# Two sum passes of a graph kernel: the edge weights move from VectorE's one-hots to ScalarE's multiply of the gathered rows

## The reference, cut to what matters

```python
# layer 1: edge_index = (row, col), 7 edge types
index = row * 7 + edge_type
mean = segment_sum(x[col], index, N * 7) / maximum(count of index, 1)[:, None]
out = mean.reshape(N, -1) @ weights
# layer 2:
h = x @ W
deg = segment_sum(ew, col, N);  dinv = where(deg > 0, rsqrt(deg), 0)
norm = dinv[row] * ew * dinv[col]
out = segment_sum(h[row] * norm[:, None], col, N) + bias
```

## Time and profile before

| | us |
|---|---|
| median of 3 runs | 9,699.5 |
| lowest, highest | 9,695.85, 9,704.59 |
| span of the profiled execution | 10,401.4 |
| of it: pass "sum1" | 3,755 to 5,010 |
| of it: pass "sum2" | 5,545 to 6,803 |
| busy: TensorE, VectorE, GpSimd, ScalarE | 6,311.5, 4,856.6, 4,458.2, 2,031.2 |

### The profile page before, as it was taken

One profiled execution on the slowest core, in us unless ns is written; L12 is line 12 of the kernel. 1 busy time (PEld: TensorE's weight loads), 2 busy tenths in 40 slices (PEclk: granted clock), 3 DMA queues, 4 the chain that ended last, 5 costly groups with the idle time before them and its releaser, 6 DMA issues. The chain is left out here.

```text
span 10401.4 us, 95746 instructions
## 1 busy us (share of the span) xinstructions
PE 6311.5 (61%) x28050; PEld 4795.7 (46%) x28050; DVE 4856.6 (47%) x13537; ACT 2031.2 (20%) x5038; POOL 4458.2 (43%) x4412
## 2 busy tenths in 40 slices
PE   0001115999996865454665444453965788887699
PEld 0000004888884433333443333342863676776466
DVE  7561216888884532222242222264113566666633
ACT  0000002444443210000120000012212232232322
POOL 0546772666660036666104666602020566664000
PEclk9998557999997986666676666675987777777799
DMA  0001002333330133333102333301960232222000
GB/s 12 6 1 28 7 4 71 83 83 83 83 83 14 46 108 92 94 92 92 35 11 70 94 92 92 92 18 25 316 221 27 77 81 80 80 81 64 11 13 19
DMA packets 404431, 697.45 MB, mean 67 GB/s; under 512 B 154143, under 2 KB 267784, under 8 KB 403421
## 3 DMA queue, kind: packets, MB, share of 16 engines
q0 software_dynamic: 206848, 480.68, 17.1%
q1 hardware_dynamic: 197076, 210.68, 6.3%
HBM read 631.46 MB, written 59.47 MB: 66 GB/s over the span
## 5 line engine op out<-in xcount | busy, mean ns | idle before, releaser
L658 POOL DMA_INDIRECT att_rows<-el_table,dst_order_row x1520 | 1589.4, 1046 | 1067.4 <-issue 387.0
L641 PE MATMUL sum_sum<-sum_rows,sum_hot 128*125 128x256 f32 x3520 | 1227.5, 487 | 1291.4 <-issue 817.1
L641 PEld LDWEIGHTS sum_sum<-sum_rows,sum_hot 128*125 128x125 f32 x3520 | 824.8, 240 | 1694.4 <-issue 1540.9
L602 POOL DMA_INDIRECT sum_rows<-rel_table,src_order_row x880 | 833.0, 947 | 1042.3 <-ACTq L593 629.2
L602 POOL DMA_INDIRECT sum_rows<-el_table,dst_order_row x880 | 833.0, 947 | 956.7 <-ACTq L593 543.7
L554 POOL DMA_INDIRECT dst_order_record<-records,dst_order_row x784 | 813.7, 1038 | 589.2 <-PEq L458 297.1
L624 DVE TENSOR_TENSOR gnn_acc<-gnn_acc,sum_sum 125x256 f32 x440 | 180.6, 410 | 1888.8 <-DMA ffn1e_w<-in_L_ffn_W_dram 938.7
L1136 PE MATMUL att_sum<-att_rows,att_hot 128*125 128x265 f32 x1280 | 429.3, 492 | 36.4 <-ACT att_part L1203 30.5
L800 PE MATMUL att_found<-gnn_to_dst,att_hot_t 125*128 x1760 | 437.8, 392 | 2.5 <-ACT att_hot_t L849 1.8
L658 POOL DMA_INDIRECT dst_order_record<-el_table,dst_order_row x240 | 266.1, 1109 | 400.4 <-SPq L960 240.5
L824 PE MATMUL att_sum<-att_rows,att_hot 128*125 128x261 f32 x1760 | 427.3, 385 | 2.4 <-ACT att_rows L862 2.4
(11 more groups left out here) (775 smaller groups left out, 12593.2 us busy)
## 6 DMA issues: line engine op xcount, KB each, us to landing
block_w<-in_L_ffn_W_dram SPq DMA_DIRECT2D x112, 512.0 KB, 6.3
block_w<-in_L_ffn_W_dram SPq DMA_DIRECT2D x56, 1024.0 KB
att_rows<-el_table,dst_order_row POOLq DMA_INDIRECT x1520
rel_table<-open_st SPq DMA_DIRECT2D x25, 784.0 KB
sum_rows<-rel_table,src_order_row POOLq DMA_INDIRECT x880
sum_rows<-el_table,dst_order_row POOLq DMA_INDIRECT x880
dst_order_record<-records,dst_order_row POOLq DMA_INDIRECT x784
pairs<-zeros SPq DMA_DIRECT2D x1, 7168.0 KB
```

Of the source, the lines that this page charges most:

```text
L602: nc.gpsimd.indirect_dma_start(rows[l][:, g, :], None, table, bass.IndirectOffsetOnAxis(ap=o["row"][:, k:k + 1], axis=0)).then_inc(s[f"row ...
L641: last = nc.tensor.matmul(slot(u), hot[u % HOTS_S][:, g, :], rows[l][:, g, :], start=(g == 0), stop=(g == G - 1))
L658: nc.gpsimd.indirect_dma_start(rows[l][:, g, 0:width], None, table, bass.IndirectOffsetOnAxis(ap=o["row"][:, k:k + 1], axis=0)).then_inc(s ...
```

## The change

GpSimd's loop stays. VectorE makes a unit's four one-hots in one comparison and without weights, ScalarE gets a loop: it waits for a unit's rows and multiplies each chunk's rows by the weights of its edges, in place. TensorE waits for ScalarE's new signal "weighed" where it waited for the rows.

```diff
@@ -590,7 +590,7 @@
         hot = [ctx.enter_context(nc.sbuf_tensor(f"{tag}_hot{l}", [P, G, R], F32)) for l in range(HOTS_S)]
         banks = [ctx.enter_context(nc.psum_tensor(f"{tag}_sum{l}", [R, 2, D], F32)) for l in range(SLOTS_S // 2)]
         slot = lambda u: banks[u % SLOTS_S // 2][:, u % 2, :]
-        with phase(nc, tag, "cleared", "batch_summed", "step", *[f"rows_in{l}" for l in range(LANES_S)]) as s, nc.Block() as block:
+        with phase(nc, tag, "cleared", "batch_summed", "step", "weighed", *[f"rows_in{l}" for l in range(LANES_S)]) as s, nc.Block() as block:
             @block.gpsimd
             def _(pool):
                 for u in range(UNITS_S):
@@ -610,10 +610,7 @@
                 def make_hot(u):
                     if u >= HOTS_S:
                         dve.wait_ge(s["batch_summed"], batches_of(u - HOTS_S))
-                    for g in range(G):
-                        k = u * G + g
-                        last = v.tensor_scalar(hot[u % HOTS_S][:, g, :], c["iota"][:, 0:R], o["node"][:, k:k + 1], w[:, k:k + 1], ALU.is_equal, ALU.mult)
-                    return last
+                    return v.tensor_tensor(hot[u % HOTS_S][:], row_of(c["iota"][:, 0:R], G), col_of(o["node"][:, u * G:u * G + G], R), ALU.is_equal)
 
                 def add(u, steps):
                     at = dve.value_load(o["tile"][0:1, u:u + 1], min_val=0, max_val=TILES - 1)
@@ -636,11 +633,21 @@
                 for u in range(UNITS_S):
                     l = u % LANES_S
                     pe.wait_ge(s["step"], u + 1)
-                    pe.wait_ge(s[f"rows_in{l}"], 16 * G * (u // LANES_S + 1))
+                    pe.wait_ge(s["weighed"], u + 1)
                     for g in range(G):
                         last = nc.tensor.matmul(slot(u), hot[u % HOTS_S][:, g, :], rows[l][:, g, :], start=(g == 0), stop=(g == G - 1))
                     if u % BATCH == BATCH - 1:
                         last.then_inc(s["batch_summed"], 1)
+
+            @block.scalar
+            def _(act):
+                for u in range(UNITS_S):
+                    l = u % LANES_S
+                    act.wait_ge(s[f"rows_in{l}"], 16 * G * (u // LANES_S + 1))
+                    for g in range(G):
+                        k = u * G + g
+                        last = nc.scalar.activation(rows[l][:, g, :], rows[l][:, g, :], ACT.Copy, scale=w[:, k:k + 1])
+                    last.then_inc(s["weighed"], 1)
 
 
 def load_tile(eng, o, u):
```

## The result

The changed kernel takes 9,745.6 us (9,743.2 to 9,749.0) against 9,700.9 for the kernel before (medians of four runs each): a ratio of 1.0049, 95% interval 1.0037 to 1.0061. That is 45 us slower; 9,768 was forecast, in a range of 9,699 to 9,820.

A forecast was written before the change was run, and what follows sets the result against it. The prediction took the gathers' issue on GpSimd to bound the sum passes. From 9,699.5 us it added 4 (relay) and 66 (new compares delaying gathers), less 2 (old compares): 9,768 us, range 9,699 to 9,820.

The forecast's parts named there:

- The gathers' issue on GpSimd paces the pass: Sum passes: 880 gathers at 1.25 us each make 1,100 us a pass; saving VectorE's work gives nothing by itself.
- The waits of 5.8 us: Sum passes: GpSimd's waits in one of eight units, 153 us a pass, taken as part of what profiling adds.
- The relay: ScalarE's multiply between rows and matmul: costs only where a pass drains, +4 us in two passes (0 to 8).
- The compare against the gathers: Sum passes: a running new compare holds up a gather until its end; +66 us in two passes (0 to 118).
- that one waits up to 6.5, I take 6 us: Start of a pass: one gather waits for all 11 back-to-back new compares, 6 us a pass.
- through two in a row too: Claim from an earlier trace row: a gather waits through two back-to-back compares, taking 1.42 us in place of 0.95.
- 209 compares at 0.13: Rest of a pass: 0.46 of the compares hit a gather, mean delay 0.28 us, 27 us a pass.
- the prediction's last sentence: Caveat on phase: a burst of four compares locked to the gathers by the batch signal may hit more or less.
- rival 1: Sum passes: gathers aren't delayed on the path, so about the same time, 9,704 us; chance 0.28.
- The old compare: Sum passes: removing the old compares, which slow gathers slightly, gives -2 us for both passes (0 to -12).
- The second: Rival: ScalarE's relay gets into the path, needing over 5.0 us a unit; 9,920 us at 5.5; chance 0.02.
- The third: Rival: the old compares held the gathers, 20 us a pass, and the new are free; 9,663 us; chance 0.07.

The follow-up runs named there:

- e5: The kernel before, with one-hots made for the first 14 units only and old ones used later: 9,690.1 us, ratio 0.9995.
- e0: The kernel before, unchanged, profiled a second time: 9,705.8 us, ratio 1.0001; profiled span 9,695.7 us.
- e1: The changed kernel with ScalarE's multiply kept, but VectorE making the one-hots in four TENSOR_SCALAR compares without a weight: 9,706.9 us, ratio 1.0006.
- e2: The kernel before with the new 128x500 compare in place of its four, no ScalarE multiply, weights left out: 9,734.8 us, ratio 1.0036.
- e4: The changed kernel, with VectorE's compare for unit u released when the rows of unit u-2 have landed: 9,704.8 us, ratio 1.0002.
- e8: The changed kernel with each unit's compare cut into four back-to-back TENSOR_TENSOR compares of 128x125: 9,747.3 us, ratio 1.0054.

## Why the prediction was right

*The pace.* "The gathers' issue on GpSimd paces the pass" is right: 879 steps in 1,102.7 us are 1.254 us each, and removing nearly all of VectorE's compares gives nothing (e5). The waits of 5.8 us were indeed not in the timed runs, but they aren't "part of what profiling adds" either: one profile in ten had them (e0).

*VectorE and ScalarE by themselves.* 0.67 us a unit for the compare and 1.70 for the multiplies (measured in the changed kernel at 671 ns, and 374.8 us over 220 units), neither on the path: as predicted. VectorE's busy time is 215 and 214 us a pass, below the 240 expected. The relay was put at +4 us: it lengthens the drains by 4.6 us in e1 and, with the new compare, by 6.3 in the changed kernel, and in the timed runs it can't be told from nothing (e1).

*The compare against the gathers.* The mechanism is as predicted, and the term of +66 us was too large. The new gathers are (973 - 946) x 0.88 + (976 - 946) x 0.88 = 50 us over 946 ns. Half of the 16 us is the start of a pass, "that one waits up to 6.5, I take 6 us": gathers get in between the long compares, and it is 2.0 us, 8 us less over both passes. The assumption behind it, that a gather waits "through two in a row too", was misread from one row with two compares. The second compare began at 8045.08 (0.60 us behind 8044.48), ahead of the gather at 8045.15, and the first ended just as the gather began; 0.13 us later only the second ran. The gather waited for that one alone, 0.47 us. The other half of the 16 us is the mean: 209 compares at 0.13, 27 us a pass, come out at (50 - 4) / 418 = 0.11 us each.

*How much of it is luck.* Late gathers are 193 for 440 compares, 0.44 each, where a uniform phase gave 0.46, with a mean delay of 0.27 us for the 0.28 predicted. But the phase isn't uniform: the same compares make 142 late gathers in e2 and 17 in e4. That the mean came out so near is in part luck, as the prediction's last sentence allows. And the range, 9,699 to 9,820, also holds the 9,704 of rival 1: the time alone would not have told the two apart, the gathers' rows do.

*The old compare* was worth more than the -2 us taken and inside its bounds: 950 and 949 ns against 946 are (4 + 3) x 0.88 = 6 us, and e5 gets to 946. With 50 - 6 + 6 = 50 us the sum agrees with the spans (51.5); the forecast had 68, and the timed runs say 45.

*The rivals.* The first, that the gathers aren't delayed on the path, falls with e0 and e2. The second needed ScalarE at over 5 us a unit, and it took 1.7. The third, that the old compares were what held the gathers, is out by a factor: 0.023 us each was needed, and 6 us over 1,760 are 0.003.
## What to carry to other kernels

When an instruction on an idle engine is replaced or fused, ask what it holds while it runs, and whether the engine that sets the pace needs that: here a form that takes VectorE 0.67 us in place of 1.10 costs the gathers 50 us. Look for the same pair of instructions elsewhere in the trace, as the earlier trace rows did, and read the mean and the longest duration, not the median: both medians are 946 ns. Where such a pair can't be avoided, release the one from an event with a fixed phase to the other (e4). And when a profile's span is 7% from the timed runs, take another before comparing.

## What the runs showed of the hardware

- An indirect DMA of 128 rows of 1 KB is issued in a median of 0.946 us before and after the change, and the next starts 0.30 us later. In the changed kernel one that meets a 128x500 compare with two operands in SBUF ends 0.81 to 0.84 us behind that compare's end (all 193 late ones).
- 44 compares of 128x125 with two operands in SBUF, back to back, kept one gather waiting 7.3 us (8.25 in place of 0.95, in e8); 11 of 128x500 kept none waiting longer than 0.52 us. 44 of 128x125 with one operand in SBUF and the scalar from a column kept none waiting longer than 0.12 us (e0 and e1).
- The same kernel's profiled executions spanned 10,401 and 9,696 us. In the longer one TensorE issued matmuls 2 to 3 us apart in stretches of both sum passes. Why this happened was not tried.
